# The tail of a softmax loop: where VectorE loads the block offset of the next update

## The chip, the cores and the metric

The kernel runs on one core of one Trainium2 chip. The core has TensorE (matrix products into PSUM), VectorE and ScalarE (elementwise work), GpSimd and SyncE (here they issue transfers), all with instruction streams of their own that meet only at semaphores. Time is microseconds (us) on the device for one execution, the median of several. One execution was profiled; all rows are from it.

## The reference

Two graph layers, each followed by a residual and a LayerNorm, over 6250 nodes and 100000 edges that are sorted by target. The second layer is the one at issue here:

```python
h = features @ W.T + b
e = leaky_relu(s1[src] + s2[dst], 0.01)         # s1, s2: h times two vectors, plus a bias
m = segment_max(e, src, N)
ex = exp(e - m[src])
out = segment_sum((ex / segment_sum(ex, src, N)[src])[:, None] * h[dst], src, N)
x = layernorm(x + out)
```

## The kernel before

**Tiling.** Nodes are kept in 52 blocks of 122 (`NS`, `BN`). For the second layer the edges are sorted by source block and padded, so that each group of 512 edges (four tiles of 128, `TG`) belongs to one block. Here there are 208 groups. A running softmax goes over them: every partition is one node of the block, `top` holds the running maximum, and `o_sb` (a part of `arena`) holds for every block 128 weighted sums and the sum of the weights (129 columns, `OROW`).

**A step.** In step g, GpSimd gathers the rows of later groups into `room` (four gathers a group, three where another way fetches the fourth tile, so seven for two groups). TensorE spreads the scores of group g + 2 (L1108), brings maxima back to the edges (L1119), forms the weighted sums of group g - 3 (L1129, eight matmul records), and every second step fetches the near tile (L1140). ScalarE makes penalties, exponentials and scaled rows. VectorE, the function `step1`, does in this order: `update` of group g - 5 (`LAG` = 5), `max_old`, `maximum` (L1587), four parts for the edges of group g - 2 mixed with four of the maximum, `members` (L1544), the spots' one-hot `spread` (L1629), and `near_shift` (L1638) or `near_add` (L1646) in turn.

**The update.** `update(g, k, lead)` (L1547 and on) multiplies the block's row of `o_all` by the decay and adds the new sums (L1554). Which block it is, is data: `dve.value_load` (L1549) reads the offset from `blk_i` into a register of VectorE's sequencer, and the instruction takes its address from there. It then waits for the sums (`step_done`), the decay (`decay_ready`) and the update before it (`st_ready`). TensorE in turn waits for `st_ready` before it writes a bank of sums anew.

**The tail.** The number of groups is data too, so the steps are: some unrolled ones, a loop (`Fori`), and the last 48 (`TAIL`) unrolled. In the tail's steps j = 1 to 47, `early` follows the step: the piecewise last stage of the blocks that are done (L1688, L1694, L1698, then L1702 and L1703, which are joined by a semaphore that VectorE waits for, `link`), and in the last five steps normalisations (L1706) as well. After the tail come the edge parts of the last two groups, the three updates still open, the rates of the second run of blocks with their normalisations, and the two last updates; then the last eight blocks.

**Order.** Each engine's order is the order of the program text. An engine instruction waits in its engine's queue, while the sequencer goes on; a register load or a wait that stands by itself occupies the sequencer.

Of the kernel before, what the change touches and what calls it, by code (L numbers as in the profile page):

```python
# [21 lines left out]
NS = -(-N // BN)  # L22
# [6 lines left out]
TAIL = 48  # L29
# [18 lines left out]
S1 = 8  # L48
LAG = 5
# [5 lines left out]
OROW = P + 1  # L55
# [23 lines left out]
def build(nc, x, x_t, e, src_pg, dst_pg, dst_g, rel_g, fcT, attn, WT, Wn, b, a1, a1b, a2, a2b, out):  # L79
    with ExitStack() as ctx:  # L80
        def sb(name, shape, dt=F32):
            return ctx.enter_context(nc.sbuf_tensor(name, shape, dt))
# [71 lines left out]
        blk_i = sb("blk_i", [P, G1], I32)  # L154
# [143 lines left out]
        def is_near(g):  # L298
            return g % NEAR_PER == NEAR_PER - 1 and g >= NEAR_FIRST

        def near_count(g):
            return g - (NEAR_FIRST - NEAR_PER)

        def sums_of(k):
            return (AP_[:, 0:OROW], FP[1][:, 1, 0:OROW])[k % 2]
# [866 lines left out]
        def _(dve):  # L1172
# [371 lines left out]
                v.tensor_tensor(mT[:, k % SLOTS, :], loc_row[:, k % RSLOTS, :], WP[0][:, P:P + 1].to_broadcast([P, GE]),  # L1544
                                ALU.is_equal).then_inc(mT_ready, 1)

            def update(g, k, lead):  # L1547

                r = dve.value_load(blk_i[0:1, bass.ds(g, 1)], min_val=0, max_val=NS * OROW)  # L1549
                dve.wait_ge(step_done, g + 5)  # L1550
                dve.wait_ge(decay_ready, g + 1)
                if not (lead and k == 0):
                    dve.wait_ge(st_ready, g)
                v.scalar_tensor_tensor(o_all[:, bass.ds(r, OROW)], o_all[:, bass.ds(r, OROW)], decay[:, k % SLOTS:k % SLOTS + 1],  # L1554
                                       sums_of(k), ALU.mult, ALU.add).then_inc(st_ready, 1)

            def edge_parts(g, k, lead):

                dve.wait_ge(step_done, g + 2)
                v.tensor_reduce(sm[:, :, :], back_of(k).rearrange("p (u c a) -> p u c a", c=2, a=PARTS3), AX.X,  # L1560
                                ALU.add).then_inc(sm_read, 1)

            def edge_sum(g, k, lead, at):

                dve.wait_ge(sm_read, g + 1)
                v.tensor_tensor(el[:, 0, :], sm[:, :, 0],
                                hg_all[:, bass.ds(at, 1), :, P + 1].rearrange("p o u -> p (o u)"),
                                ALU.add).then_inc(edge_summed, 1)

            def edge_lrelu(g, k, lead):  # L1570
                dve.wait_ge(edge_summed, g + 1)
                v.scalar_tensor_tensor(el[:, 1, :], el[:, 0, :], SLOPE1, el[:, 0, :], ALU.mult,
                                       ALU.max).then_inc(edge_sloped, 1)

            def edge_shift(g, k, lead):

                dve.wait_ge(edge_sloped, g + 1)
                if k >= 2 or not lead:
                    dve.wait_ge(pr_ready, g - 1)
                v.tensor_tensor(ed[:, k % 2, :], el[:, 1, :], sm[:, :, 1], ALU.subtract).then_inc(ed_ready, 1)  # L1580

            def maximum(g, k, lead):

                dve.wait_ge(pen_ready, g + 1)
                dve.wait_ge(step_done, g if not lead or k else 1)
                dve.sem_inc(dve_turn, 1)
                v.tensor_tensor_reduce(junk[:, :], pen[:, k % SLOTS, :], rows_of(k), 1.0, -BIG, ALU.add, ALU.max,  # L1587
                                       vmax[:, :]).then_inc(v_done, 1)

            def max_old(g, k, lead):  # L1590

                if k >= 1 or not lead:
                    dve.wait_ge(m_ready, g)
                v.tensor_tensor(top_old[:, :], top[:, :], start_b[:, bass.ds(g, 1)].to_broadcast([P, 2]),
                                ALU.min).then_inc(old_ready, 1)

            def max_raw(g, k, lead):

                dve.wait_ge(v_done, g + 1)
                dve.wait_ge(old_ready, g + 1)  # L1600
                v.scalar_tensor_tensor(top[:, 0:1], vmax[:, :], s1g[:, bass.ds(g, 1)], top_old[:, 0:1], ALU.add,  # L1601
                                       ALU.max).then_inc(raw_ready, 1)
# [4 lines left out]
            def max_lrelu(g, k, lead, at):  # L1607
                dve.wait_ge(raw_ready, g + 1)
                v.scalar_tensor_tensor(top[:, 1:2], top[:, 0:1], SLOPE1, top[:, 0:1], ALU.mult, ALU.max)
                v.scalar_tensor_tensor(part(at, 0), top[:, 0:1], SLOPE1, top[:, 0:1], ALU.mult,  # L1610
                                       ALU.max).then_inc(top_ready, 1)
# [15 lines left out]
            def spread(g, k, lead):  # L1627

                v.tensor_tensor(spots[k % 4], WP[0][:, 0:P].rearrange("p (o w) -> p o w", o=1).to_broadcast([P, TG, P]),  # L1629
                                ssf[:, bass.ds(g * TG, TG)].rearrange("p (u o) -> p u o", o=1)  # L1630
                                .to_broadcast([P, TG, P]), ALU.is_equal).then_inc(spots_ready, 1)
# [9 lines left out]
            def near_add(g, at):  # L1641

                dve.wait_ge(near_done, near_count(g))
                dve.wait_ge(far_loaded, near_count(g) * (16 // NEAR_PER))
                dve.wait_ge(step_done, g - 3)
                v.tensor_tensor(hg_all[:, bass.ds(at, 1), TG - 1, :].rearrange("p o k -> p (o k)"), near_p, far_rows,  # L1646
                                ALU.add).then_inc(near_added, NEAR_PER)

            def step1(g, k, lead, at, edge_at, ahead=True, near=2, near_slot=None):
                prev = None if lead and k < 2 else (g - 2, (k - 2) % S1, lead)  # L1650
                if not (lead and k < LAG):
                    update(g - LAG, (k - LAG) % S1, lead)
                max_old(g, k, lead)
                maximum(g, k, lead)
                if prev:
                    edge_parts(*prev)
                max_raw(g, k, lead)
                if prev:
                    edge_sum(*prev, edge_at)
                max_lrelu(g, k, lead, at)  # L1660
                if prev:
                    edge_lrelu(*prev)
                max_rest(g, k, lead, at)
                if prev:
                    edge_shift(*prev)
                max_out(g, k, lead, at)
                if ahead:
                    members(g + 2, (k + 2) % S1, lead and k < S1 - 2)
                if prev:
                    spread(*prev)  # L1670
                if near > 1 and is_near(k + 6 + (0 if lead else 2 * S1)):
                    near_shift(g + 6)
                if near and is_near(k + 3 + (0 if lead else 2 * S1)):
                    near_add(g + 3, (at + 3) % S1 if near_slot is None else near_slot)

            dve.wait_ge(o_zero, 1)
            dve.wait_ge(s_blk, 1)
# [33 lines left out]
            tail = dve.snap(more + (G1_LEAST - TAIL))  # L1711
            members(0, 0, True)
            members(1, 1, True)
            for k in range(S1):
                step1(k, k, True, k, k - 2)
            for g in range(S1, G1_LEAST - TAIL - S1):
                step1(g, g % S1, False, g % S1, (g - 2) % S1)
            with dve.Fori(G1_LEAST - TAIL - S1, dve.snap(more + (G1_LEAST - TAIL - S1 + D1 + 1)), D1) as i:
                half = dve.snap(i & (S1 - D1))
                other = dve.snap(S1 - 2 - half)  # L1720
                for k in range(D1):
                    step1(i + k, k, False, half + k, half + (k - 2) if k >= 2 else other + k, True, 2,
                          half + 3 if k == 0 else other - 1)
            for j in range(TAIL):
                k = j % S1
                step1(tail + j, k, False, k, (k - 2) % S1, j < TAIL - 2, (j + 3 < TAIL) + (j + 6 < TAIL))
                if j >= 1:
                    early(j - 1, tail + j)
                if j == TAIL - 6:
                    rates(1, slice(*RUNS[0]))  # L1730
                    dve.wait_ge(n_rs, 1)
                if j >= TAIL - 5:
                    for q in mine[0][2 * (j - TAIL + 5):2 * (j - TAIL + 6)]:
                        normal(q)
            for j in range(TAIL - 2, TAIL):
                last = (tail + j, j % S1, False)
                dve.wait_ge(ed_ready, tail + j)
                edge_parts(*last)
                edge_sum(*last, j % S1)
                edge_lrelu(*last)  # L1740
                edge_shift(*last)
                spread(*last)
            for j in range(TAIL - LAG, TAIL - 2):
                update(tail + j, j % S1, False)
            rates(2, slice(*RUNS[1]))
            dve.wait_ge(n_rs, 2)
            for q in mine[1]:
                normal(q)
            for j in range(TAIL - 2, TAIL):
                update(tail + j, j % S1, False)  # L1750


            def average(q0, q1):
# [54 lines left out]
```

## Time and profile before

| | |
|---|---|
| time, median of 3 runs (lowest to highest) | 2537.67 us (2537.1 to 2540.32) |
| profiled execution, its own time | 2536.95 us |
| its span, first to last instruction | 2535.1 us |
| VectorE busy over the span | 91% |
| TensorE (matmul), ScalarE, GpSimd busy | 86%, 77%, 72% |
| softmax loop's updates, first to last | 1578.8 to 2514.9 us |
| update of the tail's first step | 2258.3 us |

How to read it: busy time is the share in which an engine works on an instruction; waiting, register work and loads into registers are not counted. In the views, an engine's name with a q (DVEq) is its sequencer. DVE is VectorE, ACT is ScalarE, PE is TensorE, POOL is GpSimd. A number in brackets at the end of a row is the engine's idle time in front of that instruction and what the profile takes to have ended it. An instruction's end may lie behind the start of the next, since they overlap by some 0.08 us. L1549 is line 1549 of the kernel.

### The profile page before, as it was taken

Reading aid. Unit: us, or ns where it says so; the run is one execution under the profiler, and the core shown is the slowest. Engines: PE = TensorE matmul, PEld = TensorE weight load, DVE = VectorE, ACT = ScalarE, POOL = GpSimd, SP = SyncE. Lnnn points to the kernel's source line nnn. Section 1 sums busy time; section 2 is a strip of 40 time slices with the busy share of each in tenths; the row PEclk is TensorE's granted clock in tenths of the full one; section 3 lists DMA queues with packets and bytes.
Section 4 is the critical chain, followed back from the end, with each engine's and each line's share of the span. In section 5 each row is a group of like instructions: output and inputs, shape, how many; then the busy total and the mean of one; then the engine's idle time right before and its main releaser. Section 6 shows DMA issues by size and latency. Waiting matters only on the chain. (4 is left out here: it accounts for less than half of the span.)

```text
span 2535.1 us, 49366 instructions
## 1 busy us (share of the span) xinstructions
PE 2173.4 (86%) x12265; PEld 1562.1 (62%) x12266; DVE 2299.6 (91%) x5975; ACT 1950.8 (77%) x5574; POOL 1824.8 (72%) x1746
## 2 busy tenths in 40 slices
PE   6999999999999999999999974766667777777674
PEld 3566666666666666666666654766667666776664
DVE  9999999999999999999999986778887778888886
ACT  5788888888888888888888854777777777776666
POOL 3477777777777777777777745777777777776662
PEclk8999999999999999999999986899998888888886
DMA  4233333333333333333333324444444444443332
GB/s 139 73 101 104 104 106 101 104 103 104 105 106 102 103 103 104 105 106 101 104 102 105 105 58 98 99 100 100 98 101 99 99 100 101 98 99 86 84 82 71
DMA packets 180816, 250.92 MB, mean 99 GB/s; under 512 B 41103, under 2 KB 110172, under 8 KB 180416
## 3 DMA queue, kind: packets, MB, share of 16 engines
q1 hardware_dynamic: 125088, 145.72, 20.2%
q0 software_dynamic: 55456, 102.13, 17.1%
q8 instruction: 103, 1.69, 0.3%
q14 instruction: 169, 1.38, 0.2%
HBM read 238.37 MB, written 9.31 MB: 98 GB/s over the span
## 5 line engine op out<-in xcount | busy, mean ns | idle before, releaser
L627 POOL DMA_INDIRECT room<-in_x,pk x784 | 925.2, 1180 | 262.5 <-issue 252.5
L1010 PE MATMUL FP<-fc_sb,room 128*128 128x512 f32 x1568 | 832.4, 612 | 2.2 <-issue 2.2
L1019 PE MATMUL WP<-at_p,rel_oh 100*128 100x512 f32 x1568 | 804.2, 594 | 0.0
L671 POOL DMA_INDIRECT room<-h_rows,y x666 | 628.9, 944 | 220.5 <-issue 184.9
L754 ACT ACTIVATE w_sb<-WP 128x512 f32<-128x512 f32 x784 | 464.1, 592 | 224.9 <-PE WP L1019 219.5
L1019 PEld LDWEIGHTS WP<-at_p,rel_oh 100*128 100x128 f32 x1568 | 297.9, 190 | 376.4 <-issue 376.4
L1108 PE MATMUL FP<-ident,room 128*128 128x128 f32 x1664 | 278.2, 319 | 277.3 <-DMA room<-h_rows,y 213.9
L1359 DVE TENSOR_TENSOR z<-FP,w_sb 128x1024 f32<-128x1024 f32 x392 | 478.8, 1221 | 1.5 <-ACT w_sb L754 1.0
L1366 DVE SCALAR_TENSOR_TENSOR y<-z 128x2048 f32<-128x2048 f32 x196 | 452.2, 2307 | 0.0
L1108 PEld LDWEIGHTS FP<-ident,room 128*128 128x128 f32 x1664 | 238.0, 220 | 312.9 <-DMA room<-h_rows,y 246.0
L1010 PEld LDWEIGHTS FP<-fc_sb,room 128*128 128x128 f32 x1568 | 266.6, 190 | 43.3 <-issue 2.6
L871 ACT ACTIVATE room<-room,pr 128x129 f32<-128x129 f32 x832 | 266.6, 392 | 6.8
L852 ACT ACTIVATE accT<-accT,neg_big 128x512 f32<-128x512 bf16 x208 | 148.7, 715 | 150.6 <-DVE accT L1544 150.4
L638 POOL DMA_INDIRECT sorted_edges<-runs,spot_i x196 | 185.8, 948 | 90.4 <-issue 60.4
L761 ACT ACTIVATE boh<-arena,rank_pay 128x52 f32<-128x52 bf16 x784 | 239.7, 378 | 0.0
L1374 DVE TENSOR_TENSOR hs<-y 128x1024 f32<-128x1024 f32 x196 | 238.4, 1216 | 0.0
L1029 PEld LDWEIGHTS AP<-doh,room 128*128 128x128 f32 x1568 | 190.6, 192 | 53.5 <-DVE room L1390 53.5
L1029 PE MATMUL AP<-doh,room 128*128 128x64 f32 x1568 | 211.1, 278 | 7.1 <-DVE accT L1350 4.2
L771 ACT ACTIVATE dot<-iota_row,dloc 128x64 bf16<-128x64 f32 x784 | 206.3, 337 | 0.0
L884 ACT ACTIVATE w_sb<-boh 122x640 f32<-122x640 bf16 x100 | 73.6, 736 | 111.3 <-PE WP L1140 108.4
L878 ACT ACTIVATE boh<-w_sb,accT 122x128 bf16<-122x128 int32 x500 | 155.4, 386 | 0.0
L1587 DVE CUSTOM_DVE_ANT_0 hs<-accT,FP 128x512 f32<-128x512 f32 x208 | 142.0, 682 | 12.5 <-issue 6.0
(280 smaller groups left out, 3475.5 us busy)
## 6 DMA issues: line engine op xcount, KB each, us to landing
room<-in_e SPq DMA_DIRECT2D x196, 256.0 KB
rel_sb<-in_rel_g SPq DMA_DIRECT2D x196, 200.0 KB
z<-sorted_sources SPq DMA_DIRECT2D x208, 128.0 KB
room<-in_x,pk POOLq DMA_INDIRECT x784
room<-h_rows,y POOLq DMA_INDIRECT x666
w_sb<-far_rows SPq DMA_DIRECT2D x100, 65.0 KB
w_sb<-near_records SPq DMA_DIRECT2D x101, 61.0 KB
sorted_edges<-runs,spot_i POOLq DMA_INDIRECT x196, 2.0
```

The lines of the kernel that those rows point to most:

```text
L627: pool.indirect_dma_start(xg[:, k, u, 0:P], None, x[:, :], bass.IndirectOffsetOnAxis(ap=pk[:, g, u:u + 1], axis=0)).then_inc(xg_in[k], 16)
L671: pool.indirect_dma_start(hg[k][:, u, :], None, h_dram[:, :], bass.IndirectOffsetOnAxis(ap=sd[:, g * TG + u:g * TG + u + 1], axis=0)).then ...
L754: nc.scalar.activation(w_sb[:, u // 2, u % 2, :], WP[u % 2][:, :], ACT.Copy).then_inc(w_copied, 1)
L761: ins = nc.scalar.activation(boh[:, k % 2, u, :], onehot[:, :, bass.ds(g * TG + u, 1)].rearrange("p b o -> p (b o)"), ACT.Identity, bias=0 ...
L871: nc.scalar.activation(hg[k][:, u, 0:P + 1], hg[k][:, u, 0:P + 1], ACT.Identity, bias=0.0, scale=pr[:, k % 2, u:u + 1]).then_inc(h_scaled, 1)
L1010: mm = pe.matmul(FP[u // 2][:, u % 2, :], e_sb[:, k, u, :], fc_sb[:, :], start=True, stop=True)
L1019: mm = pe.matmul(WP[u % 2][:, :], rel_oh[:, k % 2, u * P:(u + 1) * P], at_p[:, j, :], start=(j == 0), stop=(j == 1))
L1029: pe.matmul(AP_[:, 0:W], msg[:, k % 2, u, :], doh[:, k % 2, u, :], start=(u == 0), stop=False)
L1108: mm = pe.matmul(rows_of(k)[:, u * P:(u + 1) * P], hg[k][:, u, P + 1:P + 2].to_broadcast([P, P]), ident[:, :], start=True, stop=True)
L1359: v.tensor_tensor(z[:, h, :, :], FP[h][:, :, :], w_sb[:, h, :, :], ALU.mult).then_inc(z_done, 1)
L1366: v.scalar_tensor_tensor(y[:, :, :, :], z[:, :, :, :], SLOPE0, z[:, :, :, :], ALU.mult, ALU.max).then_inc(y_done, 1)
L1374: v.tensor_tensor(hs[:, :, :], y_all[:, :, 0:D4 // 2], y_all[:, :, D4 // 2:D4], ALU.add).then_inc(hs_done, 1)
```

## The change

`block_at(g)` is split off from `update`. In the tail, `step1` calls it for the next step's update right behind `spread`, hands the register back, and the next step's `update` uses it and loads nothing. The very first step of the tail (j = 0) still loads in `update`. Behind the tail the offsets of the last four groups are loaded one after another (the fifth from last comes from step j = 47), and then the five closing updates run. The steps ahead of the tail are as before.

```diff
-            def update(g, k, lead):
-
-                r = dve.value_load(blk_i[0:1, bass.ds(g, 1)], min_val=0, max_val=NS * OROW)
+            def block_at(g):
+                return dve.value_load(blk_i[0:1, bass.ds(g, 1)], min_val=0, max_val=NS * OROW)
+
+            def update(g, k, lead, r=None):
+
+                r = block_at(g) if r is None else r
                 dve.wait_ge(step_done, g + 5)
                 dve.wait_ge(decay_ready, g + 1)
...
-            def step1(g, k, lead, at, edge_at, ahead=True, near=2, near_slot=None):
+            def step1(g, k, lead, at, edge_at, ahead=True, near=2, near_slot=None, r=None, load_next=False):
                 prev = None if lead and k < 2 else (g - 2, (k - 2) % S1, lead)
                 if not (lead and k < LAG):
-                    update(g - LAG, (k - LAG) % S1, lead)
+                    update(g - LAG, (k - LAG) % S1, lead, r)
...
                 if prev:
                     spread(*prev)
+                r = block_at(g + 1 - LAG) if load_next else None
                 if near > 1 and is_near(k + 6 + (0 if lead else 2 * S1)):
                     near_shift(g + 6)
...
+                return r
...
+            r = None
             for j in range(TAIL):
                 k = j % S1
-                step1(tail + j, k, False, k, (k - 2) % S1, j < TAIL - 2, (j + 3 < TAIL) + (j + 6 < TAIL))
+                r = step1(tail + j, k, False, k, (k - 2) % S1, j < TAIL - 2, (j + 3 < TAIL) + (j + 6 < TAIL), r=r,
+                          load_next=True)
...
+            at_last = [r] + [block_at(tail + j) for j in range(TAIL - LAG + 1, TAIL)]
             for j in range(TAIL - LAG, TAIL - 2):
-                update(tail + j, j % S1, False)
+                update(tail + j, j % S1, False, at_last[j - (TAIL - LAG)])
             rates(2, slice(*RUNS[1]))
             dve.wait_ge(n_rs, 2)
             for q in mine[1]:
                 normal(q)
             for j in range(TAIL - 2, TAIL):
-                update(tail + j, j % S1, False)
+                update(tail + j, j % S1, False, at_last[j - (TAIL - LAG)])
```

## Rows read from the trace of the kernel before

**Rows 1.** Busy us (x instructions) by stretch: PE, PEld, DVE, ACT, POOL; clock, DMA share, GB/s.

```profile
2084.00:2254.00 170.00, 126.91 (x976) 119.34 (x974) 138.86 (x692) 128.79 (x425) 128.56 (x137) 0.87 0.44 99
2335.80:2450.00 114.20, 82.39 (x550) 75.72 (x550) 95.62 (x504) 74.38 (x250) 71.26 (x77) 0.82 0.39 82
```

**Rows 2.** Line L1554, 2084 to 2254 us: count, ns min/median/max, first and last start.

```profile
L1554 DVEq FUSED_REGOPS  x39: 57/64/65, 2089.1 to 2253.7; - x39
```

**Rows 3.** Line L1554, 2266 to 2483 us; then idle us and times by what ended it.

```profile
L1554 DVEq FUSED_REGOPS  x41: 57/57/57, 2267.3 to 2477.6; - x41
...
  ACT decay L859: 28.0, 35
  issue: 2.4, 3
  PE AP L1129: 1.6, 2
  PE FP L1129: 0.8, 1
```

**Rows 4.** VectorE in order of time, 2308 to 2310 us: start, length, instruction.

```profile
2308.28 0.16 DVE L1703 RECIPROCAL rstd<-rstd 122x1 f32<-122x1 f32 x1
2309.22 0.35 DVE L1554 SCALAR_TENSOR_TENSOR arena<-arena,decay,FP 128x129 f32 x1 [0.78 <-ACT decay L859]
```

**Rows 5.** Line L1549 in the same step, 2308.25 to 2309.2 us.

```profile
L1549 DVEq ALU_OP  x1: 45/45/45, 2308.3 to 2308.3; - x1
L1549 DVEq TENSOR_LOAD <-blk_i x1: 301/301/301, 2308.4 to 2308.4; - x1
```

**Rows 6.** Line L1553 on the sequencer in the same step.

```profile
L1553 DVEq EVENT_SEMAPHORE  x1: 50/50/50, 2309.0 to 2309.0; - x1
```

**Rows 7.** TensorE in order of time, 2316 to 2323 us.

```profile
2316.97 2.07 PE L1129 MATMUL AP<-room,z 128*128 128x129 f32 x8
...
2320.94 1.13 PE L1108 MATMUL FP<-ident,room 128*128 128x128 f32 x8 [0.17 <-DVE vmax L1587]
2322.00 0.25 PE L1119 MATMUL EP<-mparts,accT 128*128 128x6 bf16 x4
2322.11 1.14 PE L1129 MATMUL FP<-room,z 128*128 128x129 f32 x8
```

**Rows 8.** VectorE in order of time: the updates of j = 1 and 44.

```profile
2262.69 0.35 DVE L1554 SCALAR_TENSOR_TENSOR arena<-arena,decay,AP 128x129 f32 x1 [0.59 <-issue]
...
2488.63 0.35 DVE L1554 SCALAR_TENSOR_TENSOR arena<-arena,decay,FP 128x129 f32 x1 [0.27 <-issue]
```

**Rows 9.** The one-hot's register step (line L1629), and VectorE's work around it.

```profile
L1629 DVEq FUSED_REGOPS  x1: 57/57/57, 2311.6 to 2311.6; - x1
...
2311.53 0.69 DVE L1544 TENSOR_TENSOR accT<-z,WP 128x512 bf16<-128x512 bf16 x1
...
2312.74 0.28 DVE L1646 TENSOR_TENSOR room<-WP,w_sb 128x130 f32<-128x130 f32 x1
```

**Rows 10.** Ahead of the tail: line L1549, then VectorE in order of time.

```profile
L1549 DVEq TENSOR_LOAD <-blk_i x1: 305/305/305, 2214.9 to 2214.9; - x1
...
2215.07 0.68 DVE L1629 TENSOR_TENSOR hs<-WP,y 128x512 f32<-128x512 f32 x1
...
2215.80 0.35 DVE L1554 SCALAR_TENSOR_TENSOR arena<-arena,decay,FP 128x129 f32 x1
```

**Rows 11.** Line L1549: all loads up to 2494 us, and two behind it.

```profile
L1549 DVEq TENSOR_LOAD <-blk_i x201: 298/304/321, 1573.1 to 2493.2; - x101
...
L1549 DVEq TENSOR_LOAD <-blk_i x1: 977/977/977, 2496.6 to 2496.6; - x1
...
L1549 DVEq TENSOR_LOAD <-blk_i x1: 925/925/925, 2507.3 to 2507.3; - x1
```

**Rows 12.** The end of the tail in order of time: VectorE, then TensorE.

```profile
2508.79 0.35 DVE L1554 SCALAR_TENSOR_TENSOR arena<-arena,decay,FP 128x129 f32 x1 [0.88 <-issue]
...
2509.28 2.06 PE L1129 MATMUL FP<-room,z 128*128 128x129 f32 x8 [2.84 <-ACT room L871]
```

## The prediction

> **What bounds the kernel now.** I began with the busy time by stretch of time, because the change touches only the last 48 steps. In the unrolled steps ahead of the tail and in the loop (first line of [rows 1]) GpSimd issues 137 gathers in 170 us, one each 1.24 us; a pair of steps needs seven of them, so 4.34 us a step, and the updates of that stretch come every (2253.7 - 2089.1) / 38 = 4.33 us [rows 2]. There the gathers set the pace and VectorE is idle 18% of the time. In the tail (second line of [rows 1]) GpSimd falls to 62% and VectorE rises to 84%: each step also carries a piece of the last stage (average, statistics, weights of one block). The updates j = 2 to 42 start at 2267.4 to 2477.7, 40 steps in 210.3 us, 5.26 us each [rows 3]. Only one idle place repeats in them: in front of the update L1554, 28.0 + 2.4 + 1.6 + 0.8 = 32.8 us over 41 updates, 0.80 us each [rows 3]. The view puts most of it down to ScalarE's decay.
>
> One step in order of time shows that this name is misleading [rows 4]. L1703 starts at 2308.28 and ends at 2308.44, and the update starts at 2309.22. What VectorE's sequencer does meanwhile stands in the rows of L1549 [rows 5]: an address sum of 45 ns from 2308.3, the load from 2308.4 (301 ns), and register work and a range check behind it, until at 2309.0 the wait instruction of L1553 comes [rows 6]. The sequencer was never waiting for another engine, it was loading. It could not have started sooner: L1703 is held by the semaphore of L1702, so the sequencer stands level with the engine there, and no work is queued that could cover the load. Nor is TensorE close: its sums for the update come a step early. Counted through, the update at 2309.22 is that of j = 10 and the eight matmuls that end at 2319.04 [rows 7] are the sums for j = 13; that update starts 3 x 5.26 us after the one at 2309.22, at 2325.0, so its sums lie ready for 6 us.
>
> **The change part by part.** *The load leaves the front of the update.* The block runs from 2308.3 to 2309.0, 0.70 us [rows 5, 6]. What stays between reciprocal and update are two waits, 2309.0 to 2309.22. So the update should start near 2308.5, straight behind the reciprocal's end at 2308.44. If the waits, which no longer share the load's address sum, need one or two sums of their own (45 ns each [rows 5]), the gain falls to 0.61; I take 0.70. For j = 2 to 42: 41 x 0.70 = 28.7 us. The update of j = 43 stands right behind the rates of the first run, with nothing to cover its load either, and gains 0.70 as well. The update of j = 1 has 0.59 us in front of it [rows 8]; it gains 0.55, as almost all is the load. At j = 44 two normalisations lie in front and cover most of the block, 0.27 us is left [rows 8], and j = 45 looks alike: together 0.5. The updates of j = 46 and 47 have none. j = 0 keeps its load in front. Together 30.5 us.
>
> *The load goes behind the spots' one-hot L1629.* There the sequencer runs ahead. In the step of 2311 it hands over the one-hot's register step at 2311.6 while L1544 has just started, and L1646, the next engine work, starts at 2312.74 [rows 9]. That is 1.1 us of cover for 0.70 us of block and the two waits in front of L1646, of some 50 ns each like that of L1553 [rows 6]. So I cost the load at nothing, hidden by L1544 and L1629. Each of the two holds the engine for 0.6 us (2311.53 to 2312.74 for both). The steps j = 46 and 47 have no L1544: there the block and its hand-overs outlast the one-hot's 0.6 us by some 0.2; I book 0.2 once, as j = 47 then waits for TensorE anyway. Does a load wait for running engine work? The steps ahead of the tail say no: one load starts at 2214.9 and takes 305 ns, across the start of L1629 at 2215.07, with L1544 running in front of it; the update starts at 2215.80, hard behind the one-hot's end, without idle time [rows 10]. Over 201 loads the longest is 321 ns [rows 11]. Against it stand two of the last seven loads, 977 and 925 ns [rows 11], both while the output is being written. Were every moved load that long, the block would be 0.70 + 0.64 = 1.34 us, and with the two waits 0.35 to 0.4 longer than the cover, so the gain would fall to 0.3 a step: that is the far end of this cost.
>
> The Trainium skill gives a floor of about 600 ns for such a load ("DMA: Bandwidth & Descriptors", section "Latency and other measured facts"). By it the block would be 1.0 us and would just fill the cover, with any jitter showing; the trace disagrees with 301 to 305 ns, and I go by the trace.
>
> *The queue past which it moves.* Behind the load on VectorE now stand the waits and the work of near_shift or near_add, then the pieces of the last stage. All are engine work that must wait for L1629 to end anyway; TensorE and ScalarE wait for none of it sooner than that. No DMA is issued by VectorE. SyncE and GpSimd are not moved.
>
> *The four loads at the end.* After the loop, the offsets of the last four groups are loaded in one go in front of the first of the five closing updates. Today that update starts at 2508.79, 0.9 us behind the one-hot's end, and TensorE's last three sums begin at 2509.28, because they wait for its count in `st_ready` [rows 12]. Each load with its block costs 0.70 us and there are three more than now: +2.1 us on the path to the end, since the three sums follow one another without a pause and the last update follows them.
>
> *What is late next.* A step becomes 5.26 - 0.70 = 4.56 us. GpSimd needs 4.34, and the steps ahead of the tail show that all engines together do hold 4.33 [rows 1, 2]. The margin is 0.22 us a step, and the tail begins with no lead of the gathers. In the first ten steps, until 10 x 0.22 us of lead are there, one group of sums at TensorE's low clock comes 2.07 - 1.14 = 0.93 us late [rows 7]: I book one such, 1 us, out of none to four.
>
> **Sum.** 30.5 - 2.1 - 0.2 - 1 = 27.2 us. The profiled execution took 2536.95 us (span 2535.1), 0.7 less than the median of 2537.67. So 2509.8 in its terms, 2510.5 against the median. Extremes of the terms: per step 0.61 instead of 0.70 takes 4 us off the gain, start-up losses another 3; a luckier end (its matmuls ran at the low clock, 2.06 instead of 1.14 us for eight, two to three times [rows 7, 12]) gives up to 3. The likeliest case alone: 2506 to 2518.
>
> **The rivals.**
> *The gathers or TensorE take over.* For it: the small margin, and half-clock stretches in every second step [rows 7]. Against it: the pace of 4.33 us ahead of the tail. If steps settle at 4.9 us, the gain is 43 x 0.36 - 2.2 = 13 us: 2524.
> *The load is stretched behind the one-hot*, as in the two long cases [rows 11]. 43 x 0.3 - 2.2 = 11 us: 2527. Against it: 201 short ones, many of them under the same L1544 and L1629.
> *It does not do what it says*: the load waits until the engine is drained, or the idle time really belongs to the decay. Then only the end changes: 2540, no change by the bound below. Against it [rows 5, 10].
> *Slower through TensorE's clock.* The tail's granted clock is 0.82 [rows 1], a mix of the two levels 1.2 and 2.4 GHz. At the low one a step costs TensorE 1.13 x 2.07 / 1.14 = 2.05 for the rows, 0.25, 2.07 for the sums, and half of ten near matmuls at 0.26 each, 1.3: 5.67 us [rows 7], more than today's 5.26. If denser work in the tail held the clock low throughout, 43 x 0.41 + 2.2 = 20 us more: 2558. It decides only once the low level holds for over four fifths of the tail; now it is about a third, and ahead of the tail, with denser work, the clock is 0.87, not less [rows 1].
>
> **How the numbers follow.** Forecast (2506 to 2518) 0.74; gathers or TensorE 0.12; stretched load 0.06; no effect 0.05; slower 0.03. The range should leave out 2 in 10: it reaches from 2505 over the forecast and the nearer half of the two middle rivals, to 2522. A measurement of this kernel can tell some 0.2% (5.1 us) from no change. Faster by more: 0.74 + 0.12 + 0.06 = 0.92. Within: 0.05. Slower: 0.03.
>
> **What the profile after would show.** In the tail the idle time before the update falls from 0.80 us to under 0.15 us, the loads still take about 0.3 us and start while the one-hot's predecessor runs, L1638 and L1646 still follow the one-hot at once, and the step is about 4.56 us; GpSimd's share in the tail rises to some 70% or more, and more of VectorE's waits carry TensorE's name. At the end four loads stand in a row in front of the first closing update. Wrong would be: idle time of 0.3 us or more behind the one-hot (stretched load), or idle time in front of the update that ends with TensorE (pace of others), or a clock well under 0.8 in the tail.

## The result, and the profile after

The changed kernel takes 2511.81 us (median of four, 2510.22 to 2512.47); the kernel before, timed beside it, 2538.92 us (four, 2537.1 to 2540.32). The ratio is 0.9893, 95% interval 0.9876 to 0.991: faster by 27.1 us. The forecast was 2510.5, by a gain of 27.2 from the 2537.67 known then. The profiled execution took 2511.91 us.

In the changed kernel the load is L1548, the update L1557, the maximum L1590, the one-hot L1632, `near_shift` L1641 and `near_add` L1649. The page after, its span and busy time by engine:

```profile
span 2510.0 us, 49367 instructions
PE 2155.5 (86%) x12265; PEld 1545.0 (62%) x12266; DVE 2298.5 (92%) x5975; ACT 1950.5 (78%) x5574; POOL 1826.6 (73%) x1746
```

**By stretch.** The changed kernel's busy time (PE, PEld, DVE, ACT, POOL; clock, DMA share, GB/s), ahead of the tail and in it; the second line answers to the second of [rows 1]:

```profile
2084.00:2254.00 170.00, 125.53 (x986) 118.35 (x986) 136.80 (x687) 127.29 (x421) 128.55 (x137) 0.88 0.43 99
2310.00:2424.00 114.00, 79.85 (x628) 73.93 (x626) 108.60 (x571) 82.86 (x282) 85.28 (x91) 0.91 0.47 97
```

Ahead of the tail nothing has moved. In the tail VectorE went from 84% to 95% busy and GpSimd from 62% to 75%. VectorE has no hole left there, but the gathers are close behind. TensorE's waits in the steps j = 2 to 42 show it (what it waited for; us in total, times, longest), first in the kernel before:

```profile
PE FP L1108 <- DVE vmax L1587: 55.8, 28, 3.3
PE FP L1108 <- DMA room<-h_rows,y: 2.7, 3, 1.8
```

and in the changed one:

```profile
PE FP L1108 <- DMA room<-h_rows,y: 33.3, 21, 2.5
PE FP L1108 <- DVE vmax L1590: 22.4, 13, 5.0
```

Before, TensorE waited almost only for VectorE; now it waits longer for the gathered rows than for VectorE.

**The line of the update**, j = 2 to 42, which answers to [rows 3] (count, ns, first and last start; then idle time and times by what ended it):

```profile
L1557 DVEq FUSED_REGOPS  x41: 57/57/57, 2269.3 to 2451.7; - x41
...
  PE FP L1129: 1.0, 1
```

The 32.8 us of idle time are down to one wait of 1.0 us, the only one long enough to be listed. The updates run from 2269.37 to 2451.80, 40 steps of 4.56 us instead of 5.26.

**One step in order of time** (VectorE of the changed kernel; start, length), which answers to [rows 4, 9]:

```profile
2303.23 0.68 DVE L1544 TENSOR_TENSOR accT<-z,WP 128x512 bf16<-128x512 bf16 x1
2303.82 0.68 DVE L1632 TENSOR_TENSOR hs<-WP,y 128x512 f32<-128x512 f32 x1
2304.43 0.22 DVE L1641 TENSOR_SCALAR w_sb<-w_sb 122x128 int32<-122x128 int32 x1
...
2305.26 0.16 DVE L1708 RECIPROCAL rstd<-rstd 122x1 f32<-122x1 f32 x1
2305.49 0.35 DVE L1557 SCALAR_TENSOR_TENSOR arena<-arena,decay,FP 128x129 f32 x1
```

The update starts 0.23 us after the start of the reciprocal (0.94 in [rows 4]), and `near_shift` starts hard behind the one-hot. The load is still made. VectorE's sequencer, line L1548, in a step just before the one shown, over the steady tail, and in the batch behind it (count; ns least, median, most):

```profile
L1548 DVEq TENSOR_LOAD <-blk_i x1: 311/311/311, 2298.8 to 2298.8; - x1
...
L1548 DVEq TENSOR_LOAD <-blk_i x43: 299/305/316, 2268.0 to 2459.2; - x43
...
L1548 DVEq TENSOR_LOAD <-blk_i x4: 300/354/981, 2480.2 to 2483.0; - x4
```

**The end** (VectorE and TensorE in order of time), which answers to [rows 12]:

```profile
2480.07 0.69 DVE L1632 TENSOR_TENSOR hs<-WP,y 128x512 f32<-128x512 f32 x1
2483.86 0.35 DVE L1557 SCALAR_TENSOR_TENSOR arena<-arena,decay,FP 128x129 f32 x1 [3.10 <-issue]
2484.36 2.06 PE L1129 MATMUL FP<-room,z 128*128 128x129 f32 x8 [5.05 <-DVE arena L1557]
```

The four loads stand between the last one-hot and the first closing update: 3.10 us of idle time instead of 0.88, and TensorE's wait grew from 2.84 to 5.05.

**Where the time went**, between starts of updates in the two profiled executions:

| stretch | before, us | after, us | difference | forecast |
|---|---|---|---|---|
| up to j = 0 | 2258.30 | 2261.51 | +3.2 | 0 |
| j = 0 to 2 | 9.09 | 7.86 | -1.2 | -1.25 |
| j = 2 to 42 | 210.27 | 182.43 | -27.8 | -28.0, +1 for start-up |
| j = 42 to 45 | 16.41 | 14.76 | -1.65 | -1.2 |
| j = 45 to 47 | 7.93 | 8.31 | +0.4 | +0.2 |
| j = 47 to the last update | 12.92 | 14.92 | +2.0 | +2.1 |
| last update to the end | 20.2 | 20.2 | 0 | 0 |

The 3.2 us in the first row lie where both kernels run the same instructions. They are scatter of executions: in the twelve profiled executions of kernels that are alike up to there, the update of j = 0 starts between 2258.3 and 2262.9 us. So the two profiled executions differ by 28.3 us from j = 0 on, and by 25.1 in all.

### The profile page after: what moved, and what is told of

It is laid out like the page before. It is cut to its first block, busy times and chain, and to the rows that moved or that the text cites. A ratio compares the mean times of both kernels' runs of the same rounds, so it can differ in the third digit from the quotient of the medians.

```text
span 2510.0 us, 49367 instructions
## 1 busy us (share of the span) xinstructions
PE 2155.5 (86%) x12265; PEld 1545.0 (62%) x12266; DVE 2298.5 (92%) x5975; ACT 1950.5 (78%) x5574; POOL 1826.6 (73%) x1746
## 4 chain that ended last, share of the span: by engine, by line
DVE 41%; issue 25%; POOL 14%; PE 8%; DVEq 6%; DMA 6%; ACT 0%; POOLq 0%; SPq 0%; ACTq 0%
DVE y L1366 17%; POOL room L671 14%; DVE hs L1374 10%; DMA room<-h_rows,y 6%; DVEq L1346 4%; DVE room L1390 4%; PE FP L1108 3%; PE AP L1129 2%; DVE accT L1350 2%; DVE z L1359 1%; PE FP L1129 1%; DVEq L1548 1%; DVE joh L1340 1%; DVE room L1382 1%; DVE arena L1211 0%
## 5 line engine op out<-in xcount | busy, mean ns | idle before, releaser
L1590 DVE CUSTOM_DVE_ANT_0 hs<-accT,FP 128x512 f32<-128x512 f32 x208 | 141.9, 682 | 12.3 <-issue 6.0
```

## The experiments

My theory: in the sequencer's stream, what stands behind a register load isn't handed to VectorE until the load's block of 0.70 us is through. So the load costs what the queued engine work in front of it doesn't cover, and nothing when L1544 and the one-hot lie in front. Rivals: the gain came from something else that the rewriting changed; the place in the step doesn't matter as long as it isn't in front of the update; the load is waited for like engine work of ScalarE, as the view's name (decay) says. Diffs are against the changed kernel unless they say otherwise. The kernel before was timed beside each of them, so its median differs a little from one to the next.

### One more load, in the old place

Against the kernel before, in the 48 steps of the tail (the lines that hand `twice=True` to `update` are left out here):

```diff
             def update(g, k, lead, twice=False):
+                if twice:
+                    dve.value_load(blk_i[0:1, bass.ds(g, 1)], min_val=0, max_val=NS * OROW)
                 r = dve.value_load(blk_i[0:1, bass.ds(g, 1)], min_val=0, max_val=NS * OROW)
```

> The kernel before, with a second, unused load of the same offset in front of each of the 48 updates of the tail. It measures the price of one load in the place it was moved from. Theory: the place has no cover, so 0.70 us for j = 2 to 43 and for j = 1, about 0.7 for j = 44 to 47 less what the normalisations cover, and somewhat under 0.70 at j = 0: 46 x 0.70 = 32 us, 2571 us. Rival (the idle time belongs to the decay, or to TensorE, and the load lies beside it): no change, 2539.

Measured: 2568.91 us, ratio 1.0121 [1.0105, 1.0136], 30.0 us more than before (2538.96). The steps j = 2 to 42 went from 5.26 to 5.91 us. The update's line in that kernel, with the idle time by what ended it:

```profile
L1556 DVEq FUSED_REGOPS  x41: 64/64/64, 2270.3 to 2506.5; - x41
...
  ACT decay L859: 39.4, 28
  PE AP L1129: 13.0, 9
  issue: 6.7, 4
```

59.1 us over 41 updates are 1.44 each, 0.64 more than the 0.80 of [rows 3]. Nothing of ScalarE or TensorE was changed, yet the idle time put down to ScalarE's decay grew from 28.0 to 39.4, and that put down to TensorE's sums from 2.4 to 13.0. These names are those of the last wait met after the load, not the cause. The doubled load costs about what the moved one gave back.

### The load at other places of the step

The same load and hand-over, one place further forward, between `members` (L1544) and the one-hot:

```diff
+                r = block_at(g + 1 - LAG) if load_next else None
                 if prev:
                     spread(*prev)
-                r = block_at(g + 1 - LAG) if load_next else None
```

> The change, with the load one place earlier: between the member mask L1544 and the one-hot, not behind the one-hot. Theory: the sequencer reaches the place just as the mask starts, so the cover is the mask alone, 0.6 us for a block of 0.70 us and the hand-over of the one-hot: the one-hot starts 0.15 to 0.2 us late in each step, 46 x 0.17 = 8 us more than the change: 2520 us. Rival (any place that is not directly in front of the update is as good): 2512.

Measured: 2520.48 us, ratio 0.9928 [0.9911, 0.9944]; the step is 4.70 us, 0.14 more than in the changed kernel. VectorE of this kernel, two steps in order of time:

```profile
2307.79 0.69 DVE L1544 TENSOR_TENSOR accT<-z,WP 128x512 bf16<-128x512 bf16 x1
2308.61 0.69 DVE L1632 TENSOR_TENSOR z<-WP,y 128x512 f32<-128x512 f32 x1
...
2312.47 0.68 DVE L1544 TENSOR_TENSOR accT<-z,WP 128x512 bf16<-128x512 bf16 x1
2313.56 0.69 DVE L1632 TENSOR_TENSOR z<-WP,y 128x512 f32<-128x512 f32 x1 [0.41 <-issue]
```

The one-hot starts 0.82 us behind the start of L1544 where it otherwise follows in 0.6: the block is 0.70 us and L1544 covers 0.6. Such a delay of 0.2 us is too short for a bracket; the second step shows a longer one. Over the tail the distance is 0.74 us in the median and 1.17 at most; why it varies no run shows.

One place further forward still, in front of `members`:

```diff
+                nxt = block_at(g + 1 - LAG) if load_next else None
                 if ahead:
                     members(g + 2, (k + 2) % S1, lead and k < S1 - 2)
                 if prev:
                     spread(*prev)
-                r = block_at(g + 1 - LAG) if load_next else None
+                r = nxt
```

> The change, with the load another place earlier: in front of the member mask, behind the last small operation of the maximum. There the sequencer stands level with the engine, as in front of the update. Theory: almost the whole block shows in front of L1544, 0.60 to 0.70 us a step (the small operation in front covers up to 0.1), so the gain of the steps is gone: 2539 to 2542 us, as the kernel before. Rival (what matters is that the load is away from the update, because there it holds up a wait for TensorE or ScalarE): 2512.

Measured: 2543.01 us, ratio 1.0012 [1.0002, 1.0021]; before was 2539.67 here. The step is 5.19 us, so all but 0.07 of the 0.70 us a step is gone. This kernel's waits of VectorE in the tail (total, times, longest), and one step:

```profile
DVE accT L1544 <- issue: 24.2, 40, 1.0
...
2310.23 0.16 DVE L1626 TENSOR_TENSOR mparts<-rest,mparts 128x1 bf16<-128x1 f32 x1
2310.95 0.69 DVE L1544 TENSOR_TENSOR accT<-z,WP 128x512 bf16<-128x512 bf16 x1 [0.56 <-issue]
```

No idle time in front of the update is long enough to be listed any more; the hole has moved to where the load went, 0.6 us in each of 40 steps. This is the clearest run of the study: same load, same count, same hand-over, and the hole follows it. The rival "anywhere but in front of the update" is out.

Two loads behind the one-hot, the second doing nothing:

```diff
                 r = block_at(g + 1 - LAG) if load_next else None
+                r = block_at(g + 1 - LAG) if load_next else None
```

> The change, with the offset loaded twice in a row behind the one-hot in each of the 48 steps (the second value is used). Theory: the cover there is 1.1 us (the member mask and the one-hot, handed over before the load) less two waits of 0.05; two blocks take 1.4 us, so 0.35 to 0.45 us of idle time appears behind the one-hot in each step, 48 x 0.4 = 19 us: 2530 us. Rival 1, nothing is really hidden and the gain comes from elsewhere: 0.70 a step, 34 us, 2545. Rival 2, the cover is far larger than thought: nothing, 2512.

Measured: 2531.37 us, ratio 0.9969 [0.9958, 0.9981]; the step is 4.98 us, 0.42 more than in the changed kernel. VectorE's waits in this kernel's tail, and two places in order of time:

```profile
DVE w_sb L1641 <- issue: 5.9, 19, 0.6
DVE room L1649 <- PE FP L1129: 4.4, 12, 0.7
DVE room L1649 <- issue: 2.7, 7, 0.7
...
2312.60 0.29 DVE L1649 TENSOR_TENSOR room<-WP,w_sb 128x130 f32<-128x130 f32 x1 [0.71 <-PE FP L1129]
...
2317.44 0.23 DVE L1641 TENSOR_SCALAR w_sb<-w_sb 122x128 int32<-122x128 int32 x1 [0.27 <-issue]
```

The cover L1544 and one-hot, 1.2 us, holds one block of 0.70 but not two of 1.40. The rest comes out at the next engine work, here 0.27 us of idle time in front of `near_shift` and 0.71 in front of `near_add`, with a wrong name (TensorE's sums) on part of it. The two rows are unlike, but over the tail `near_shift` starts 0.98 us and `near_add` 1.03 us behind the start of the one-hot (medians), against 0.60 for both in the changed kernel: 0.4 us more, as the step says. With one load the cover was enough, with less to spare than a second load needs.

### The end alone

Against the kernel before: the steps as before, but all five closing updates' offsets loaded in one go behind the last one-hot.

```diff
+            at_last = [block_at(tail + j) for j in range(TAIL - LAG, TAIL)]
             for j in range(TAIL - LAG, TAIL - 2):
-                update(tail + j, j % S1, False)
+                update(tail + j, j % S1, False, at_last[j - (TAIL - LAG)])
```

> The kernel before, with nothing changed in the 48 steps; only the five closing updates have all their offsets loaded in one go in front of the first. This does the closing part of the change alone. My theory: four loads more in front of the first closing update, 4 x 0.70 = 2.8 us later to the end: 2541.7 us (ratio 1.001). The step 0.80 us of idle time in front of each update stays. Rival (the gain of the change comes from a different packing of the program, not from the moved load): then this kernel, whose instruction order is also new, would show part of the 27 us gain.

Measured: 2541.43 us, ratio 1.0011 [1.0002, 1.002], 2.5 us more than before; the step is 5.25 us, so without the moved load nothing is gained. TensorE's third sum from the end in this kernel:

```profile
2513.29 2.06 PE L1129 MATMUL FP<-room,z 128*128 128x129 f32 x8 [5.76 <-DVE arena L1557]
```

5.76 us of waiting instead of 2.84 [rows 12]: four loads more in front of the update that it waits for.

The changed kernel without the batch (j = 47's load stays, the last four are each made in front of their update):

```diff
-            at_last = [r] + [block_at(tail + j) for j in range(TAIL - LAG + 1, TAIL)]
+            at_last = [r] + [None] * (LAG - 1)
```

> The change, but the last four closing updates load their offsets in front of themselves again; only the first of the five has its offset from the last step. My theory says that the batch of four loads in front of the first closing update stands on the path to the end: in the changed kernel that update starts 3.10 us behind the one-hot's end, and TensorE idles 5.05 us in front of its last three sums. Without the batch the update follows the one-hot at once, so the three sums and the end come 3 us earlier: 2508.8 us against 2511.8 (ratio to the kernel before 0.988). Rival: the last three sums wait for ScalarE's scaled rows (2482.92 for the last group in the changed kernel), not for the update: then at most 0.5 us is gained, 2511.3 us.

Measured: 2510.13 us (2507.38 to 2512.55), ratio 0.9891 [0.9876, 0.9906]. Once more, on one chip with the changed kernel itself:

> The changed kernel itself, run beside the next two, so that differences of 2 to 4 us can be seen on one chip: 2512 us.

> The kernel of e1 again, beside the changed kernel on the same chip. In its profile the way from the update of the last step to the last update is 12.4 us, in the changed kernel 14.9. Theory: 2.5 us less than the changed kernel, 2509.5. Rival: the closing part differed by TensorE's clock alone, then the medians agree within 0.5 us.

Measured: the changed kernel 2513.18 us (2511.37 to 2514.7), ratio 0.9893 [0.9877, 0.991]; without the batch 2511.7 (2510.82 to 2513.74), ratio 0.9887 [0.9871, 0.9904]. The medians of the last two differ by 1.5 us in the expected direction, but the intervals overlap: the times alone don't settle it. The traces do for the place itself. From the update of j = 47 to the last one it is 12.40 and 12.39 us without the batch, 14.92 and 15.08 with it. VectorE and TensorE at the end of the first of these kernels:

```profile
2478.29 0.69 DVE L1632 TENSOR_TENSOR hs<-WP,y 128x512 f32<-128x512 f32 x1
2478.90 0.34 DVE L1557 SCALAR_TENSOR_TENSOR arena<-arena,decay,FP 128x129 f32 x1
2479.38 2.06 PE L1129 MATMUL FP<-room,z 128*128 128x129 f32 x8 [1.86 <-DVE arena L1557]
2480.34 0.35 DVE L1557 SCALAR_TENSOR_TENSOR arena<-arena,decay,AP 128x129 f32 x1 [1.11 <-issue]
```

The first closing update stands hard behind the one-hot, the sum starts at once, and the 1.11 us of idle time in front of the second update lie beside that sum of 2.06 us. They are that long because the second update's load is one of the long ones, 1167 ns.

Then the first closing update moved ahead of the edge parts of the last two groups, on top of that:

```diff
+            update(tail + (TAIL - LAG), (TAIL - LAG) % S1, False, r)
             for j in range(TAIL - 2, TAIL):
                 ...
-            at_last = [r] + [block_at(tail + j) for j in range(TAIL - LAG + 1, TAIL)]
-            for j in range(TAIL - LAG, TAIL - 2):
+            at_last = [r] + [None] * (LAG - 1)
+            for j in range(TAIL - LAG + 1, TAIL - 2):
```

> As e1 (each of the last four closing updates loads in front of itself), and in addition the first closing update moved ahead of the edge parts of the last two groups. Theory: in e1 TensorE still idles 1.86 us between the sums of the fifth and the fourth last... it waits for the first closing update, 2478.90, while its own work before ended at 2477.52 and ScalarE's rows at 2476.70. With the update ahead of the edge parts TensorE's last three sums start when ScalarE's rows and its own earlier sums are there: 1.8 us sooner than in e1, limited by the rows of the last two groups (2479.74, 2481.15), which come 0.4 us later as the update now stands in front of their edge parts. So 1.3 to 1.8 us less than e1, and 3.5 to 4.5 less than the change: 2508 us. Rival: the 0.4 us in front of the edge parts is on the path as well, as ScalarE works without pause there, and nothing is won over e1.

Measured, on the chip of the last two: 2509.78 us (2507.3 to 2511.58), ratio 0.988 [0.9864, 0.9897]. From j = 47's update to the last one it is 12.39 us, exactly as without the move, so this expectation failed in its place. TensorE in this kernel:

```profile
2480.84 2.06 PE L1129 MATMUL AP<-room,w_sb 128*128 128x129 f32 x8 [1.86 <-DVE arena L1557]
```

The third sum from the end does start early, at 2477.05, but the next one then waits the same 1.86 us for the second closing update, which stands behind the last one-hot and a load of its own, of 1224 ns. The wait moved by one update. How much of it would go with a load of 0.3 us, no run shows. The median 1.9 us below its neighbour isn't explained by the trace and isn't told from scatter.

### What bounds the tail now

The load behind the one-hot in the unrolled steps ahead of the tail too, on top of the kernel without the batch:

```diff
+            r = None
             for g in range(S1, G1_LEAST - TAIL - S1):
-                step1(g, g % S1, False, g % S1, (g - 2) % S1)
+                r = step1(g, g % S1, False, g % S1, (g - 2) % S1, r=r, load_next=g + 1 < G1_LEAST - TAIL - S1)
```

> The kernel of e1, with the load behind the one-hot also in the unrolled steps 9 to 143 ahead of the loop, not only in the tail. Theory: there the gathers set the pace, 4.34 us a step, and VectorE has 0.5 us of waits a step, so 135 loads moved give nothing that can be told from none: 2508.8 us, within 3. Rival (VectorE's sequencer also limits those steps, as the idle time there is partly put down to issue): up to 0.2 us a step, 27 us: 2482.

Measured: 2509.92 us, ratio 0.9888 [0.9872, 0.9905], as without it (2510.13). The update's line of this kernel from 1620 to 2254 us, idle time by what ended it:

```profile
  PE FP L1129: 31.9, 25
  issue: 3.2, 8
```

In the kernel before, the same stretch had 39.4 us behind TensorE's sums and 35.7 us of `issue`, in 64 places. So 40 us of idle time went from the critical-looking place, and the pace stayed: 4.38 us a step, 4.37 in the kernel before. The gathers set it there, as TensorE's waits in the same stretch of this kernel say:

```profile
PE FP L1108 <- DMA room<-h_rows,y: 181.5, 121, 3.2
```

In the kernel before these were 179.0 us. The same edit is worth 0.70 us a step in the tail and nothing ahead of it.

Last, VectorE's work of the last stage out of the tail:

```diff
-                    dve.wait_ge(n_avg, q + 1)
-                    v.bn_stats(stats[:, q, :], xn[:, q, :]).then_inc(n_stat, 1)
+                    dve.sem_inc(n_stat, 1)
...
-                    link(v.tensor_scalar(rstd[:, i:i + 1], o_sb[:, i, P:P + 1], 1.0e-30, None, ALU.max))
-                    v.reciprocal(rstd[:, i:i + 1], rstd[:, i:i + 1]).then_inc(n_weight, 1)
+                    dve.sem_inc(n_weight, 1)
```

(and the average of the same blocks likewise; this kernel leaves out part of the last stage's work and works on old numbers instead)

> The change, with the averages, statistics and weights of the first 44 blocks left out of the tail (only their signals are given), so the last stage works on old numbers. It takes 0.7 to 0.75 us of VectorE's work from each of some 44 steps and asks what is next behind VectorE. Theory: the gathers' 4.34 us a step are the floor, so of 4.56 us only 0.22 a step goes: 10 us, 2502 us. Rival 1 (VectorE alone counts, with a floor of 3.85 us): 32 us, 2480. Rival 2 (TensorE or the start of the tail already set the pace of 4.56): nothing, 2512.

Measured: 2505.56 us, ratio 0.9868 [0.9852, 0.9885]. The step is 4.39 us on average (3.7 to 6.9 us singly), and from 1620 to 2254 us it is 4.39 in the same execution. Waits of VectorE in this kernel's tail:

```profile
DVE arena L1557 <- PE FP L1129: 13.3, 7, 3.1
DVE room L1649 <- PE WP L1140: 5.6, 10, 1.4
DVE arena L1557 <- issue: 3.6, 15, 0.4
```

Now VectorE waits for TensorE, up to 3.1 us at once, and TensorE in the same stretch for nothing but gathered rows:

```profile
PE FP L1108 <- DMA room<-h_rows,y: 34.5, 22, 3.3
PE FP L1108 <- DMA room<-h_rows,idx: 20.1, 13, 3.3
```

Without that work the tail runs at the gathers' pace. So the changed kernel stands 0.17 us a step above the floor. The 4.34 forecast for the floor was a little low: from 1620 to 2254 us the thirteen profiled executions run at 4.36 to 4.40 us a step. At 0.05 a step that is 2 us over the tail, more than half of the 3.6 us by which this time lies above its expectation.

## Why the prediction was right

**What the hole was.** Right. It was the load's block, not ScalarE's decay: twice the load made the decay's share grow with nothing done to ScalarE, and moving the load moved the hole.

**0.70 us a step.** Right: 4.56 us forecast, 4.56 found. That it fits to the hundredth is luck: the six profiled executions whose tail has these same steps run at 4.54 to 4.59, and the 4.56 here has one late sum of 1.0 us in it; without it the 40 steps gained 0.72 us each. The choice of 0.70 over 0.61 was right too: the update starts 0.23 us behind the reciprocal's start, and the waits left there need no longer.

**The load behind the one-hot costs nothing.** Right. `near_shift` follows the one-hot with no gap, and all 43 loads take 299 to 316 ns there. The rival of the stretched load is out for the steady tail. Where a load was stretched, in step j = 45 (1082 ns), 0.27 us of idle time came out behind the one-hot, near the 0.35 to 0.4 us that the prediction priced:

```profile
2470.20 0.18 DVE L1693 BATCH_NORM_AGGREGATE mv<-stats 122x2 f32<-122x6 f32 x1 [0.27 <-issue]
```

The margin behind the claim was one-sided, as the other places showed: with only L1544 as cover 0.14 us a step comes out, with none of the two nearly all (0.63 us).

**The other updates.** j = 0 to 2: 1.25 forecast, 1.2 found. j = 42 to 45: 1.2 forecast, 1.65 found. j = 46 and 47: 0.2 lost forecast, 0.4 found. Only 0.14 of that lies in the step without L1544, which the forecast meant; 0.24 lies in the step j = 45 with the stretched load.

**What is late next.** Right in kind: VectorE stays the bound (95% busy), and the gathers come just behind. Their floor is some 4.39 us, not 4.34. The rival by which gathers or TensorE take over at 4.9 us did not happen: with VectorE's work left out, when only they were left to set the pace, the step was 4.39. The 1 us of start-up loss, for one late sum of TensorE, was a term for something that differs between executions. In this one the first steps lost nothing (4.34 and 4.33 us for j = 2 and 3), and the one late sum came at j = 20 with 1.0 us. In the second profiled execution of the changed kernel the first two steps took 5.22 and 5.24 us, with two waits of VectorE for TensorE:

```profile
2271.65 0.29 DVE L1649 TENSOR_TENSOR room<-WP,w_sb 128x130 f32<-128x130 f32 x1 [0.80 <-PE WP L1140]
2277.77 0.35 DVE L1557 SCALAR_TENSOR_TENSOR arena<-arena,decay,FP 128x129 f32 x1 [0.99 <-PE FP L1129]
```

In two further executions with these same tail steps VectorE waited 1.67 and 2.27 us at once in the step of j = 4. So the term was right in kind, and its size changes from execution to execution.

**The end.** Right: +2.1 forecast, +2.0 found; the batch alone cost 2.5 us in its run. The reading that TensorE's last three sums wait for the first closing update, against the name in the view of before (ScalarE), was right too: the first of them starts 0.48 to 0.50 us behind the start of that update in the kernel before, the changed one, the one with the batch alone and the one without it.

**Slower by the clock.** Wrong in direction as well as improbable, below. [rows 1] already had the higher clock in the denser stretch, as the prediction said itself.

**The sum.** The terms are right in kind and near in size. That 27.2 us meet 27.1 in the medians is luck: from j = 0 on the two profiled executions differ by 28.3 us, 1.1 more than the sum, and the times of one kernel scatter over some 3 us.

## What to carry to other kernels

Idle time in front of an instruction that uses an address from data is first to be looked for in the sequencer's rows of its own engine, whatever releaser the view names. A register load belongs behind the longest engine instructions that are queued without a wait in between (here 1.2 us of cover for a 0.70 us block), and it pays only where that engine sets the pace (here 0.70 us a step in the tail and nothing ahead of it). Loads gathered in one batch in front of an instruction that another engine waits for come out in full (here 2.2 us for three more); in front of each user they hid beside the other engine's work.

## What the runs showed of the hardware that I had not expected

**The clock rose in the denser tail.** The stretch of the updates j = 2 to 42, as a whole, in the kernel before and then in the changed one (columns as in [rows 1]):

```profile
2267.40:2477.70 210.30, 150.52 (x1012) 138.54 (x1011) 174.19 (x918) 138.98 (x460) 136.62 (x145) 0.82 0.40 85
```

```profile
2269.40:2451.80 182.40, 127.92 (x1015) 118.77 (x1014) 174.31 (x917) 137.25 (x460) 136.83 (x146) 0.92 0.45 97
```

The same 40 steps keep VectorE busy for 174.2 and 174.3 us, but TensorE for 150.5 and then 127.9, at a granted clock of 0.82 and 0.92; in the second execution of the changed kernel it was 132.9 us at 0.89. Over the runs the order holds but for 0.01 between neighbours, all from 2310 to 2424 us: 0.78 with 5.91 us a step, 0.83 and 0.84 with 5.26 and 5.25 (the kernel before, and the one with the batch alone), 0.83 with 5.19, 0.84 with 4.98, 0.88 with 4.70, 0.88 and 0.91 for two executions of the changed kernel, 0.89 to 0.91 for four executions of kernels that differ from it only at the end or ahead of the tail, 0.91 with 4.39. So tails of shorter steps had more of the high level, not less. The length of the step alone doesn't set it, though: in the kernel before, ahead of the tail and at one pace of about 4.34 us a step, the clock was 0.97 from 1700 to 1800 us and 0.86 from 2100 to 2200. What set it there no run separates. The kernel's time gained nothing from it that the sum needed, since TensorE isn't the bound of the tail. My rival had the wrong sign because it took denser work for a reason to slow down. The granted clock is a mix of the two levels 1.2 and 2.4 GHz, so 0.82 is 64% of the stretch at the high one and 0.92 is 84%. The Trainium skill says that the default state is the throttled one and that activity releases it ("TensorE: Matmul & The Clock Gate", section "Part 1: The HAM clock gate"); among the tails these traces agree, with 0.78 at 5.91 us a step and 0.91 at 4.39; the two stretches ahead of the tail, 0.97 and 0.86 at one pace, they don't explain by it.

**Single register loads take over three times as long near the end.** In the kernel before, 201 loads take 298 to 321 ns [rows 11], and in the changed one the 43 of the steady tail 299 to 316. In the changed kernel one of the eight from 2464 us on takes 1082 ns and another one 981; in the kernel before there were 977 and 925 [rows 11]. Without the batch it was again one under the last steps and one in the closing part: 1055 and 1167 ns, with the early closing update 1062 and 1224. Under the last steps it cost 0.27 us, the part that the two instructions in front didn't cover; in the closing batch it is in full on the way of TensorE's last sums. The transfers of the output come in bursts, and the long loads lie in them. In the changed kernel, the stretch of the 1082-ns load, that of the 981-ns load, and that of a load of 302 ns between two bursts (columns as in [rows 1]):

```profile
2468.80:2470.00 1.20, 1.20 (x9) 1.20 (x10) 1.13 (x2) 0.64 (x2) 0.00 (x0) 0.52 0.79 226
2480.20:2481.20 1.00, 0.00 (x0) 0.00 (x0) 0.56 (x1) 0.97 (x5) 0.00 (x0) 0.50 0.76 222
2477.00:2477.50 0.50, 0.39 (x5) 0.40 (x6) 0.50 (x2) 0.47 (x2) 0.00 (x0) 0.50 0.00 0
```

The DMA engines' share is 0.79 and 0.76 with the long loads and 0.00 with the short one. In the steady tail, at a share of 0.45 and 97 GB/s over the whole, no load took over 316 ns. But the next two loads in the second burst took 407 and 302 ns, so a burst alone doesn't make a load long. That the output's transfers are the cause is argued from the place; no run separates it.
